# Gated cross-attention expert layer with a LoRA mixture: Gram products in two PSUM banks, one scale per expert for the second and third expert, and a new order of VectorE's first operations

## What is computed

```python
x = x + tanh(g_xattn) * xattn(layernorm(x), itok, ctx, ctx, ctx)
x = x + tanh(g_ffn)  * ffn(layernorm(x), W_base, b_base, A_s, B_s, A_r, B_r, W_router, b_router)
# xattn, per expert e, for its own rows:  z = h @ ctx[e].T ; y = (silu(z) * z) @ ctx[e].T
# ffn: base product + shared LoRA + the two best of six routed LoRA experts, weighted
```

## Time and profile before

| | |
|---|---|
| runs | 202.42, 202.99, 203.41 us; median 202.99 |
| profiled execution | 201.75 us, of which the span from first to last instruction is 199.9 us |
| mean granted TensorE clock | 0.987 of full speed |
| busy share of the span | TensorE 93%, VectorE 73%, GpSimd 57%, ScalarE 56% |
| chain that ended last | 81% TensorE, 5% GpSimd, 4% VectorE, 3% DMA |

### The profile page before, as it was taken

How to read it: one execution, slowest core, us unless ns; L and a number is a source line. 1 busy time by engine, 2 the same in 40 slices (tenths; PEclk the granted TensorE clock), 3 DMA queues, 4 the chain that set the end, 5 groups by cost and what they waited for, 6 DMA issues and landing times.

```text
span 199.9 us, 3786 instructions
## 1 busy us (share of the span) xinstructions
PE 186.0 (93%) x1089; PEld 107.6 (54%) x1089; DVE 145.8 (73%) x424; ACT 111.7 (56%) x208; POOL 114.3 (57%) x190
## 2 busy tenths in 40 slices
PE   6895889799999999999999999999999999999970
PEld 2472354344444444444444446567778777787750
DVE  4918979979766667899877665766887887787470
ACT  4540958835375774466666547154765777567310
POOL 5581873895276654124377755274877776866441
PEclk9969999999999999999999999999999999999998
DMA  3998236599899999356569999477599898899851
GB/s 89 368 293 273 85 105 159 108 256 110 201 189 208 174 245 210 69 105 117 106 149 205 202 242 209 83 185 162 90 129 141 116 151 117 115 141 134 129 86 75
DMA packets 59827, 31.63 MB, mean 158 GB/s; under 512 B 53105, under 2 KB 53105, under 8 KB 59810
## 3 DMA queue, kind: packets, MB, share of 16 engines
q1 hardware_dynamic: 54994, 18.58, 47.0%
q0 software_dynamic: 4816, 12.85, 29.8%
HBM read 10.71 MB, written 7.86 MB: 93 GB/s over the span
## 4 chain that ended last, share of the span: by engine, by line
PE 81%; POOL 5%; DVE 4%; DMA 3%; issue 2%; ACT 2%; POOLq 1%; SPq 0%
PE y_ps L782 8%; PE actT_ps L782 8%; PE z_ps L782 6%; PE ffn_b L782 6%; PE ffn_b L764 6%; PE ffn_a L764 5%; PE actT_ps L787 4%; PE y_ps L787 4%; PE z_ps L787 3%; PE ffn_b L787 3%; DMA ct_stage<-ct 3%; PE ffn_b L768 3%; PE z_ps L764 3%; PE ffn_a L768 3%; PE y_ps L764 3%
## 5 line engine op out<-in xcount | busy, mean ns | idle before, releaser
L504 POOL DMA_INDIRECT out<-scaled,row_index x14 | 22.4, 1597 | 11.3 <-ACT scaled L613 4.6
L396 POOL TENSOR_SCALAR var_eps<-item_stats_t 128x1 f32<-128x1 f32 x19 | 6.8, 360 | 34.3 <-DVE item_stats_t L1116 34.0
L433 POOL DMA_INDIRECT xg<-x_rows,row_index x19 | 22.5, 1184 | 5.5 <-issue 4.2
L568 ACT ACTIVATE act_split<-act 128x512 f16<-128x512 f32 x19 | 11.9, 628 | 15.7 <-DVE act L1141 15.6
L764 PE MATMUL ffn_a<-w_split,hT 128*128 128x316 f16 x88 | 18.8, 298 | 0.0
L764 PE MATMUL ffn_b<-w_split,hT 128*128 128x314 f16 x88 | 18.4, 296 | 0.0
L446 POOL DMA_INDIRECT out<-xg,row_index x14 | 14.8, 1054 | 5.3 <-issue 3.0
L576 ACT ACTIVATE h<-xg,item_centre,item_rstd 128x512 f32<-128x512 f32 x18 | 14.4, 801 | 5.0 <-POOL item_centre L406 4.9
L782 PE MATMUL y_ps<-ct_split,actT 128*128 (+1 forms) x72 | 17.0, 379 | 0.0
L782 PE MATMUL actT_ps<-ct_split,actT 128*128 (+1 forms) x72 | 17.0, 379 | 0.0
L598 ACT ACTIVATE expd<-logits,neg_max 128x6 f32<-128x6 f32 x16 | 4.8, 299 | 19.7 <-DVE neg_max L1286 19.7
(11 more groups left out here) (225 smaller groups left out, 478.9 us busy)
## 6 DMA issues: line engine op xcount, KB each, us to landing
ct_stage<-ct SPq DMA_DIRECT2D x4, 1024.0 KB, 7.5
w_stage<-w_ffn SPq DMA_DIRECT2D x4, 315.0 KB, 3.7
hT<-h_split SPq DMA_TRANSPOSE x30, 3.7
xg<-x_rows,row_index POOLq DMA_INDIRECT x19, 4.0
actT<-act_split SPq DMA_TRANSPOSE x19, 4.0
out<-xg,row_index POOLq DMA_INDIRECT x16, 3.3
up_stage<-w_up SPq DMA_DIRECT2D x1, 224.0 KB
out<-scaled,row_index POOLq DMA_INDIRECT x14
```

What stands on the lines that cost most here:

```text
L433: nc.gpsimd.indirect_dma_start(cols(xg, q), None, x, bass.IndirectOffsetOnAxis(row_index[:, q:q + 1], 0)).then_inc(x_landed[q], 16)
L504: nc.gpsimd.indirect_dma_start(out, bass.IndirectOffsetOnAxis(row_index[:, q:q + 1], 0), scaled[t % 3][:], None, compute_op=ALU.add).then_ ...
L568: nc.scalar.activation(act_split[q % 2][:, 0:D], act[:], ACT.Copy).then_inc(act_hi_ready, 1)
```

## The change

The second expert's Gram product goes to another bank (`y_ps`, which is not used otherwise before `product_y(0)`); the bank table is `gram_banks`. `trace(1)` then waits for its own Gram product alone. Experts 1 and 2 get a total of one column each, and a scale each. The `keep_warm` counts become 2, 1, 2 and 5 in place of 5, 3 and 8. On VectorE the first operations are put in a new order.

```diff
--- before.py
+++ after.py
@@ -30,7 +30,7 @@
 EPS = 1e-5
 TOP_K = 2
 WARM_EARLY = (6, 7, 6)
-WARM_UP = (5, 3, 8)
+WARM_UP = (2, 1, 2, 5)
 WARM_BETWEEN = 3
 EXTRA_AT = 1
 EXTRA_ADD_AT = 11
@@ -187,7 +187,7 @@
         sort_ps, perm_ps = ffn_a[0], ffn_a[1]
         z_banks = (z_ps, ffn_b[1])
         warm_ps = actT_ps
-        gram_ps = ffn_b[0]
+        gram_banks = {1: ffn_b[0], 2: y_ps, 3: ffn_b[0]}
         squares_ps = ffn_a[1]
         first_total_ps = hT_ps
         TOTALS_AT = 0
@@ -734,7 +734,7 @@
                 blocks = KC * D // P
                 for b in range(blocks):
                     at = upper[:, b * P:(b + 1) * P]
-                    last = nc.tensor.matmul(gram_ps[:, (e - 1) * P:e * P], at, at, start=(b == 0),
+                    last = nc.tensor.matmul(gram_banks[e][:, (e - 1) * P:e * P], at, at, start=(b == 0),
                                             stop=(b == blocks - 1))
                 last.then_inc(gram_done, 1)
 
@@ -751,12 +751,15 @@
             total(first_total_ps[:, 0:1], ct_squares[:, 0:1], ct_squares[:, S:S + 1])
             gram(1)
             keep_warm(WARM_UP[0])
+            pe.wait_ge(rows_ready, 1)
+            pe.wait_ge(traced, 1)
+            total(total_of(1, 1), ct_squares[:, 1:2])
+            keep_warm(WARM_UP[1])
             gram(2)
-            keep_warm(WARM_UP[1])
-            pe.wait_ge(rows_ready, 1)
+            keep_warm(WARM_UP[2])
             pe.wait_ge(traced, 2)
-            total(total_of(1, 2), ct_squares[:, 1:3])
-            keep_warm(WARM_UP[2])
+            total(total_of(2, 1), ct_squares[:, 2:3])
+            keep_warm(WARM_UP[3])
 
             def ffn_hi_passes(ps, turn, rhs, k):
 
@@ -1011,9 +1014,9 @@
 
             def trace(e):
 
-                dve.wait_ge(gram_done, max(e, 2))
-                nc.vector.scalar_tensor_tensor(ct_junk[:, (e - 1) * P:e * P], gram_ps[:, (e - 1) * P:e * P], 1.0, ident[:], ALU.mult,
-                                               ALU.mult, accum_out=column(ct_squares, e)).then_inc(traced, 1)
+                dve.wait_ge(gram_done, e)
+                nc.vector.scalar_tensor_tensor(ct_junk[:, (e - 1) * P:e * P], gram_banks[e][:, (e - 1) * P:e * P], 1.0,
+                                               ident[:], ALU.mult, ALU.mult, accum_out=column(ct_squares, e)).then_inc(traced, 1)
 
             def ct_scales(total, first, count, turn):
 
@@ -1204,12 +1207,13 @@
             product_scales(0, 1)
             trace(1)
             ct_lo(0, 0)
+            ct_scales(squares_ps[:, TOTALS_AT + 1:TOTALS_AT + 2], 1, 1, 2)
+            first_rows(0)
+            trace(2)
             ct_lo(0, 1)
-            trace(2)
-            first_rows(0)
-            ct_scales(squares_ps[:, TOTALS_AT + 1:TOTALS_AT + 3], 1, 2, 2)
+            ct_scales(squares_ps[:, TOTALS_AT + 2:TOTALS_AT + 3], 2, 1, 3)
+            first_norm()
             first_rows(1)
-            first_norm()
             ct_lo(1, 0)
             hT_lo(0)
             ct_lo(1, 1)
@@ -1223,7 +1227,7 @@
             trace(3)
             first_rows(4)
             hT_lo(2)
-            ct_scales(squares_ps[:, TOTALS_AT + 3:TOTALS_AT + 4], 3, 1, 3)
+            ct_scales(squares_ps[:, TOTALS_AT + 3:TOTALS_AT + 4], 3, 1, 4)
             ct_lo(2, 1)
             activate(1)
             first_rows(5)
```

## The result

Four runs of the changed kernel took 199.55 to 201.05 us, median 200.53; four of the kernel before, beside them, 202.42 to 203.41, median 203.05. The ratio is 0.9874, 95% interval 0.9828 to 0.992. The profiled execution took 199.55 us (201.75 before), its span 197.8 (199.9).

What follows compares the result with a forecast made beforehand. TensorE was taken as bound by waits in the first 40 us, caused by VectorE's late trace: -3.2 us at item 0, 0.6 lost on GpSimd, -2.6 at item 2, giving 200.4 us against the median 202.99; range 199.5 to 201.0.

Steps and rivals of the forecast that it cites:

- -2.6 at item 2: Item 2's transposition on TensorE comes at 26.7 instead of 29.23, 2.6 us earlier by the prediction's sum.
- item 2's date is carried to the end: Everything behind item 2 on TensorE is a queue without dates of its own, so the 2.6 us reach the end.
- trace(1) now stands at 12.29 and ct_lo(0,0) at 12.51: On VectorE, no longer waiting for the second Gram product, ct_lo(0,0) starts 2.8 us earlier than before.
- The removed warming matmuls cost nothing as long as the clock stays up: On TensorE ten warming matmuls replace sixteen at no cost, since each removed one stood ahead of a wait.
- Rival D: Slower: TensorE's clock falls with fewer warming matmuls, z(0) and z(1) cost 3.8 us more; +0.2, 203.2 us; chance 0.03.
- The third gather ends at 14.70: On GpSimd the third gather starts inside ct_lo(0,0) and is held by it, ending at 14.70, not 13.73.
- Root 0, said to be held to 17.1: On GpSimd item 0's root meets ct_lo(0,1) and is ready 0.7 us after its end at 16.4.
- The 0.53 between the two scale instructions: VectorE's unexplained idle time inside the scale, taken as not recurring at the first scale; 0 to 0.5 us kept for the range.
- A: The fourth gather loses its race with ct_lo(0,1) and waits for its end; gain only 1.4, 201.6 us; chance 0.17.
- B: A gather that is first holds VectorE off, ct_lo(0,1) waits until 15.95; gain only 1.8, 201.2 us; chance 0.06.
- C: Slower: the fourth expert's load, asked for 1 us later, lands late; up to +1.3, 204.3 us; chance 0.06.
- E: A transfer further on keeps its date and the gain is given back; 203.0 us; chance 0.08.

Runs made afterwards that it cites:

- early warming: Matmuls of 256 columns behind the first twelve permutation matmuls and two of 512 behind the last, added to four kernels; on the changed kernel 200.08 us, ratio 0.9913.
- third experiment: The changed kernel with item 1's statistics ahead of item 0's normalization again: 199.86 us, ratio 0.986 to the kernel before.
- fourth experiment: The changed kernel with item 2's statistics moved ahead of ct_lo(1,1): 200.36 us, ratio 0.9897 to the kernel before.
- the last kernel of the study: The changed kernel with VectorE's old order (own bank and split scales kept) and more warming matmuls ahead of the first total: 198.90 us, ratio 0.9847 to the kernel before.

## Why the prediction was right, and which of its steps were not

**The date and the total.** Forecast 200.4, measured 200.53; item 2 at 26.7, measured 27.05; -2.6 at item 2, measured -2.18. The step on which it rests, that item 2's date is carried to the end, holds to 0.1 us. That the total fits to 0.1 is in part luck. The -2.6 is 2.5 by the sum's own dates (29.23 to 26.7); the profiled execution came 0.35 later than forecast (199.55 for 199.2), and the median lay 0.98 above it where the forecast had put 1.24.

**The cause.** The step "trace(1) now stands at 12.29 and ct_lo(0,0) at 12.51" is the change: without the own bank the trace stays late and little moves (the order alone, 0.9961), and with it alone the gain is 1.0%; with early warming it is 1.4%, and the warming by itself makes 0.2%, not told from nothing. One part of the change was not run alone: fewer warming matmuls ahead of the second Gram product. But with early warming the kernel before had that product waiting 0.50 us for its load, to 13.00, and the trace at 14.45, and it gained only those 0.2%; without the own bank fewer warming matmuls could hardly have brought it earlier. The size of the step was 0.5 too good: 12.81 and 13.02. ScalarE's squares were 0.15 later in this execution, and the total ahead of the first Gram product took 1.01 at the lower clock, for 0.62.

**The clock.** "The removed warming matmuls cost nothing as long as the clock stays up": it did not stay up, and the second Gram product took 1.91 in place of the 1.08 of the sum, so ct_lo(0,1) started at 16.25, not 15.1. Rival D's sign, a clock digit below 9 in the fourth slice, is there (8), but its price, which it puts in z(0) and z(1), was not paid: the clock was up again before item 0's transposition. Early warming shows that at item 2 the lower clock costs the changed kernel little (26.89 against 27.05 and 26.92).

**GpSimd.** "The third gather ends at 14.70" failed in the profile: trace(1) was late by more than the margin, ct_lo(0,0) began behind the gather, and the hold fell on the fourth, 0.14 us in place of some 0.95. The fourth load was asked for at 15.27, not 16.1. Root 0, said to be held to 17.1, was free (ready at 16.59). In the six other executions profiled with both the own bank and item 0's statistics ahead of ct_lo(0,1) the first trace came at 11.4 to 11.9, the third gather was held, 1.19 to 1.47 us long, and so was root 0, ready at 17.4 to 17.5: the step is right where its dates are, and it is this execution that is the exception. So two errors, a slow Gram product (VectorE done with the second scale at 17.7, not 16.7) and holds that did not happen, cancelled in part: item 0 at 18.30 for 17.7. From there the chain went as worked out: item 1's centre held by ct_lo(1,1), sixth gather unhindered (1.04), seventh held by ct_lo(2,0).

**Smaller terms.** Item 0's rows, "by 13.9", landed at 14.3 to 14.7 where VectorE had to wait for them, 4.2 to 4.7 us after the first gather's start, not 3.6. Of the first eight slices, read as all below 9, the third and the seventh are at 9. The 0.53 between the two scale instructions, taken as not recurring, did not recur.

**The rivals.** A did not happen in the profile; in the last kernel of the study its hold did, 1.15 us, at little cost. B fell: ct_lo(0,0) started 0.24 after a gather and lasted its 1.28. By the rule of the Trainium skill ("SBUF — State Buffer", "Who interferes with whom") that whoever comes first keeps the other out, it would have waited until 13.73; the trace disagrees. C and E did not occur.

**What the prediction did not see** is which part earns the gain. It treated the new order and the split scale as parts of one path. The profiles show the order to help item 0 only while the second Gram product is late: at the lower clock item 0's statistics go ahead of the wait for it (18.30 against 18.78 in the old order), and item 2 comes out even (27.05 and 27.00). With the clock up, and the runs side by side, the order costs 1.2 us; without early warming the two orders' ratios (0.9874 new, 0.9828 old) have intervals that overlap. One thing this does not explain: six of the changed kernel's own runs, with a mean granted clock of 0.977 or less, took a median of 199.7, ten at 0.98 or more 200.6, while item 2's date was nearly the same in every profile. The split scale gives nothing that can be measured in time with the clock up (198.90 and 198.82). At the lower clock the bank alone was 1.0 behind at item 2; by the timelines about half of that is the later Gram product and half the idle time inside the scale of two columns.

## What to carry to other kernels

A wait for two results where one would do can be removed with another bank, and that alone may hold the whole gain; test it alone before adding an order that fits it. An order of work is tuned to the dates it was made for: ask what it does when the wait it fills is short. And before splitting a term on a tenth of a microsecond, look whether the clock it assumes is granted in that stretch.

## What the runs showed of the hardware

**GpSimd behind VectorE.** In these profiles every gather that started 0.2 us or more inside a ct_lo (two inputs in SBUF) ended 0.81 to 0.92 us after the end of that instruction; two that started 0.02 and 0.07 us after a ct_lo were not held (0.95 and 1.04 us long), one that started 0.03 us into the second of two ct_lo back to back was (2.04). One that started first was not held (12.78 above, 0.95 us long) and did not hold the ct_lo (1.28 us). Not foreseen: a gather that started inside item 0's normalization, which reads one tile in SBUF and two columns, was held as well (17.15 to 18.31 above, 0.88 after 16.88 + 0.55 = 17.43).

**An idle half microsecond.** Between `ct_root` and `ct_scale` VectorE stood idle 0.53 to 0.54 us in every kernel profiled with a total of two columns (18.81 to 19.50 in the order alone, 17.57 to 18.24 in the bank alone), and not in one with totals of one column (14.22 to 14.41). The cause is open.

**The clock at the start** differs between executions of one kernel: the changed one ran at the lower level from 9.5 to 16.3 us in one profile, and stood at the higher from 7 to 18 us in the profiles of the third and fourth experiment, which differ from it only in VectorE's order later on. The mean granted clock of the changed kernel's runs lay between 0.972 and 0.994. TensorE did much the same either way ahead of the first total. Where the clock fell, the last matmuls of 19 columns took 1.06 us (ten of them, to 9.5), and a wait of 0.55 us followed; in the third experiment, where it did not fall, they took 0.81 us (eight), and the wait was 0.31. What decides is open.
